# Key's rope sum moved from VectorE to GpSimd, and new orders on SyncE, ScalarE, VectorE and GpSimd in an attention block

## The reference

```python
q = einsum('bsd,ed->bse', x, Wq).reshape(bsz, seqlen, 32, 128)   # 32 query heads
k, v = ... the same with Wk, Wv, 8 key heads
q = _rope(_rmsnorm(q, q_norm_w), pos)       # rope: t * cos + swapped(t) * sin
k = _rope(_rmsnorm(k, k_norm_w), pos)
k_all = concatenate([kc, k], axis=1)        # 512 cached rows, 128 new ones
v_all = concatenate([vc, v], axis=1)
scores = where(valid, einsum('bqhd,bkhd->bhqk', q, k_all) * SCALE, -1e30)
o = einsum('bhqk,bkhd->bqhd', softmax(scores), v_all)
return einsum('bse,de->bsd', o, Wo)
```

## Time and profile before

| | |
|---|---|
| median of 3 runs | 1407.14 us (1397.35 to 1407.36) |
| profiled execution | 1401.18 us, its span 1399.4 us |
| busy in the span | PE 89%, VectorE 74%, ScalarE 60%, GpSimd 67% |
| granted TensorE clock, mean | 0.963 |

### The profile page before, as it was taken

How to read it: one execution, slowest core, us unless ns; L and a number is a source line. 1 busy time by engine, 2 the same in 40 slices (tenths; PEclk the granted TensorE clock), 3 DMA queues, 4 the chain that set the end, 5 groups by cost and what they waited for, 6 DMA issues and landing times.

```text
span 1399.4 us, 23898 instructions
## 1 busy us (share of the span) xinstructions
PE 1243.0 (89%) x6856; PEld 1012.9 (72%) x6856; DVE 1042.1 (74%) x2452; ACT 846.4 (60%) x2441; POOL 943.2 (67%) x659
## 2 busy tenths in 40 slices
PE   6799997789989999999898899899989898998878
PEld 4677765577777777777677777777767777777768
DVE  3578665587777777887787778777877788777766
ACT  2677775556665666665655566666565666565641
POOL 1566564566876788777766786688668766876652
PEclk9899999899999999999999999999999999999999
DMA  7565552446555655555555555555555555545551
GB/s 255 186 220 218 224 216 53 119 109 151 120 117 118 152 121 126 135 130 120 121 128 125 117 128 126 130 122 121 128 129 121 121 130 127 127 115 123 123 153 60
DMA packets 336036, 191.32 MB, mean 137 GB/s; under 512 B 149153, under 2 KB 320162, under 8 KB 334882
## 3 DMA queue, kind: packets, MB, share of 16 engines
q1 hardware_dynamic: 334896, 189.63, 52.5%
q10 hardware_dynamic: 1010, 0.17, 0.1%
HBM read 101.66 MB, written 37.75 MB: 100 GB/s over the span
## 4 chain that ended last, share of the span: by engine, by line
PE 29%; POOL 27%; DMA 13%; issue 9%; DVE 7%; SPq 7%; ACT 6%; DVEq 0%; POOLq 0%; ACTq 0%
POOL b_p_l L1732 13%; DMA b_moved<-b_blk_first 12%; SPq L1254 7%; PE ps L1290 4%; ACT b_p_h L1493 4%; PE ps L1291 4%; PE ps L1292 4%; POOL b_v_l L1723 4%; POOL b_ra L1719 3%; DVE b_blk_first L1608 3%; PE ps L247 2%; POOL b_w_l L1694 2%; PE ps L1358 2%; DVE b_sm L1595 2%; PE ps L306 2%
## 5 line engine op out<-in xcount | busy, mean ns | idle before, releaser
L1732 POOL TENSOR_TENSOR b_p_l<-b_moved,b_p_h 128x1280 fp32r<-128x1280 f32 x128 | 380.9, 2976 | 292.7 <-ACT b_p_h L1493 292.5
L1487 ACT ACTIVATE b_sm<-b_sm,b_mn 128x640 f32<-128x640 f32 x256 | 212.3, 829 | 98.6 <-DVE b_mn L1595 94.0
L1493 ACT ACTIVATE b_p_h<-b_moved 128x1280 fp32r<-128x1280 f32 x128 | 163.2, 1275 | 134.3 <-DMA b_moved<-b_blk_first 111.1
L1595 DVE CUSTOM_DVE_ANT_0 b_sm<-ps,mask_row,b_rstd 128x640 f32<-128x640 f32 x256 | 222.1, 868 | 7.4 <-PE ps L1292 6.7
L1290 PE MATMUL ps<-b_w_h,x1t_h 128*128 128x512 f32 (+1 forms) x512 | 190.2, 372 | 24.1 <-DVE b_qt_l L1582 24.0
L1290 PE MATMUL ps<-b_kt_h,b_qt_h 128*128 128x320 f32 x512 | 166.6, 325 | 35.4 <-DVE b_kt_l L1587 34.4
L1624 DVE SCALAR_TENSOR_TENSOR b_hacc<-ps,b_ri,b_hacc 128x512 f32<-128x512 f32 x248 | 182.7, 737 | 4.3 <-PE ps L1292 3.9
L1291 PE MATMUL ps<-b_w_l,x1t_h 128*128 128x512 f32 (+1 forms) x512 | 183.9, 359 | 0.0
L1292 PE MATMUL ps<-b_w_h,x1t_l 128*128 128x512 f32 (+1 forms) x512 | 181.8, 355 | 0.0
L1291 PE MATMUL ps<-b_kt_l,b_qt_h 128*128 128x320 f32 x512 | 158.1, 309 | 0.0
L1292 PE MATMUL ps<-b_kt_h,b_qt_l 128*128 128x320 f32 x512 | 158.0, 309 | 0.0
(11 more groups left out here) (174 smaller groups left out, 3333.4 us busy)
## 6 DMA issues: line engine op xcount, KB each, us to landing
b_moved<-b_blk_first SPq DMA_DIRECT2D x256, 160.0 KB, 3.3
b_moved<-b_blk_second SPq DMA_DIRECT2D x256, 160.0 KB, 3.3
kv_of_batch<-in_kv SPq DMA_DIRECT2D x128, 256.0 KB
b_ck<-kv_of_batch SPq DMA_DIRECT2D x64, 256.0 KB, 4.2
b_cv<-kv_of_batch SPq DMA_DIRECT2D x256, 64.0 KB, 2.3
raw<-in_w SPq DMA_DIRECT2D x32, 384.0 KB, 4.7
raw<-in_wo SPq DMA_DIRECT2D x32, 256.0 KB, 4.0
a_xt<-in_xt SPq DMA_DIRECT2D x8, 256.0 KB, 6.9
```

The costliest lines, as they stand in the source:

```text
L1487: act.activation(sm[:, h % 2], sm[:, h % 2], ACT.Exp, bias=mn[:, m.b % 2, h:h + 1], scale=-1.0, accum_out=rs[:, m.b % 2, h:h + 1]).then_in ...
L1493: act.activation(pair_of(p_h, pair), moved_pair(pair), ACT.Copy).then_inc(mh_sb, 1)
L1595: dve.tensor_tensor_reduce(sm[:, h % 2], score_row(h), mask_row[:, m.b], rstd[:, m.b % 4, h:h + 1], -MASKED, ALU.add, ALU.min, mn[:, m.b % ...
L1732: pool.tensor_tensor(pair_of(p_l, pair), moved_pair(pair), pair_of(p_h, pair), ALU.subtract).then_inc(ml_sb, 1)
```

## The change

Four edits, all in stage 2 (the first one also in the hand-over from stage 1, for item 0).

1. The key's rope sum `key_sum` leaves VectorE's list, where it stood right behind `new_values(one)`, and joins GpSimd's, behind `low_probs(last, 1)`.
2. SyncE issues `blocks_across(m, 1)` right behind `blocks_across(m, 0)`; key rows, weights and value rows come behind both.
3. ScalarE: `exponent(m, 3)` goes ahead of `output(last)`, and `new_keys(one)` and `cache_values(one)` ahead of `high(m, 0)`. VectorE: `turn_blocks(m, 3)` goes ahead of `output(last)` and `invert(last)`.
4. GpSimd: `cache_values(one)` goes ahead of `low_probs(m, 0)`.

```diff
@@ SyncE
             def slot(m, one, two, last):
                 blocks_across(m, 0)
+                blocks_across(m, 1)
                 if two:
                     key_rows(two)
...
-                blocks_across(m, 1)
                 if two:
                     value_rows(two)
@@ ScalarE
                     turned_key(one)
+                exponent(m, 3)
                 if last:
                     output(last)
-                exponent(m, 3)
-                high(m, 0)
                 if one:
                     new_keys(one)
                     cache_values(one)
+                high(m, 0)
@@ VectorE
-            def key_sum(m):
-                dve.wait_ge(kab_sb, m.n + 1)
-                dve.tensor_tensor(kb[:], ka[:], kb[:], ALU.add).then_inc(kab2_sb, 1)
...
                     new_values(one)
-                    key_sum(one)
                 minima(m, 2)
...
                 turn_blocks(m, 2)
+                turn_blocks(m, 3)
                 if last:
                     output(last)
                     invert(last)
-                turn_blocks(m, 3)
@@ GpSimd
+            def key_sum(m):
+                pool.wait_ge(kab_sb, m.n + 1)
+                pool.tensor_tensor(kb[:], ka[:], kb[:], ALU.add).then_inc(kab2_sb, 1)
...
                     low_probs(last, 1)
+                if one:
+                    key_sum(one)
                 if m.b == 6:
                     q_weights(m.g + 1, range(2, KT))
...
-                low_probs(m, 0)
                 if one:
                     cache_values(one)
+                low_probs(m, 0)
                 if two:
                     rope_queries(two)
```

More of the change, by code:

```diff
@@ L619, in x1_rest @@
                                   x1t_h[:, bass.ds(d, 1)].rearrange("p b k s -> p (b k s)"), ALU.subtract).then_inc(xl_sb, 1)
-            next_products, next_values, next_key_sum, next_queries, next_keys, next_minima, next_low_weights, next_low_kv_weights = ahead
+            next_products, next_values, next_queries, next_keys, next_minima, next_low_weights, next_low_kv_weights = ahead
             def slot(b):
@@ L678, in slot @@
                     next_values(Item(0, 0))
-                    next_key_sum(Item(0, 0))
                 if inside(b + 1):
@@ L749, in with_bias @@
                 pool.tensor_tensor(xb[:, b % 2], xin[:], b_dense[:], ALU.add).then_inc(xb_sb, 1)
-            next_q_weights, next_kv_weights, next_queries, next_rms, next_cache_keys, next_cache_values = ahead
+            next_q_weights, next_kv_weights, next_queries, next_rms, next_key_sum, next_cache_keys, next_cache_values = ahead
             def slot(b):
@@ L782, in slot @@
                     next_rms(Item(0, 0))
+                    next_key_sum(Item(0, 0))
                 if b == LAST:
@@ L1674, in low_kv_weights @@
                 dve.tensor_tensor(w_l[:, :, cols], raw[:, :, cols], w_h[:, :, cols], ALU.subtract).then_inc(wkvl_sb, 1)
-            vector_first(dve, (rope_products, new_values, key_sum, queries, new_keys, minima, low_weights, low_kv_weights))
+            vector_first(dve, (rope_products, new_values, queries, new_keys, minima, low_weights, low_kv_weights))
             slots(dve, slot)
@@ L1760, in _ @@
             pool.wait_ge(const_sb, 1)
-            gpsimd_first(pool, (q_weights, kv_weights, rope_queries, rms, cache_keys, cache_values))
+            gpsimd_first(pool, (q_weights, kv_weights, rope_queries, rms, key_sum, cache_keys, cache_values))
             slots(pool, slot)
```

## The result

The changed kernel takes 1282.82 us (median of 4 runs, 1280.65 to 1286.00); the kernel before took 1407.25 us beside it (1397.35 to 1416.34). The ratio is 0.912, with a 95% interval of 0.905 to 0.918. The profiled execution took 1286.00 us, its span 1284.2.

What follows compares the result with a forecast made beforehand. The prediction took a ring of waits (15.75 us a slot) as the bound, TensorE (14.8) right below, and VectorE's key-sum stalls third. 1401.2 - 47 (stalls) - 44 (shorter ring) = 1310 us; eight in ten between 1286 and 1352.

Steps and rivals of the forecast that it cites:

- T: Start of the four transposes of the turned queries (turn_q, line 1318) on TensorE; marks each slot in stage 2.
- ordinary slots: Stage 2 slots of batches 0, 2 to 5 and 7; forecast to fall from 15.75 to 14.8 us, 46 counted.
- Batches 1 and 6: Stage 2 slots: +0.2 us x 8 in batch 6, set by GpSimd, and -0.3 x 8 in batch 1; dropped.
- Part 1: Key sum moves from VectorE to GpSimd; its stalls behind GpSimd go and count one to one: 47 us gained.
- Part 2: Cache values go into GpSimd's idle time, new keys come earlier: 15.75 - 14.8 = 0.95 us a slot, 44 us.
- the ring: T-to-T waits: head 1's transpose, pair 0's transfers, high part, GpSimd's low part, cache values, queries' rope sum; 15.75 us.
- TensorE's floor: TensorE's own work in one of the ordinary slots, 15.75 us less holes of 0.72 and 0.24: 14.8 us.
- Part 3: SyncE issues both pairs ahead of key rows, weights and value rows; pair 1 lands 1.6 us earlier, counted as nothing.
- (b): More than forecast from pair 0's landing, batch 1's clock and batch 7: 0.4 us in 60 slots, 1286; chance 0.1.
- (a): Only the stall goes, as late transfers eat the ring's 0.3 us slack: 1354 us; chance 0.2 (up to 1358).
- (c): The stall moves to another VectorE instruction with two SBUF inputs instead of going: 1357 to 1401 us; chance 0.06.
- (d): Slower: new ring through key sum, exponent 3 and pair 1, if pair 1 lands late: 1458 us; chance 0.04.

Runs made afterwards that it cites:

- the two extra sums: Changed kernel with two more 128x128 additions on GpSimd behind the key's sum in every slot but the first, results unread: 1292.90 us, ratio 0.914.
- the orders alone: Changed kernel with the key's sum back on VectorE, all other reorderings kept: 1348.24 us, ratio 0.962 to the kernel before.
- the fastest kernel: Changed kernel with key and value weights' low part on VectorE, and batch 1's output-weight pieces moved behind GpSimd's key sum or to VectorE: 1265.47 us.

## Why the prediction was right, and where it fell short

**Where the missing 24 us are.** Between the T of item 2 and that of item 63 the prediction had 47 + 44 = 91 us, all in ordinary slots. Measured, the ordinary slots gave 106.6 us, 16 more. Batches 1 and 6, put at -1 us and dropped, gave 4. The remaining 4.5 us lie outside: 1.6 ahead of the T of item 2 and 2.8 behind that of item 63, and their cause is open.

**Part 1, the sum leaves VectorE: right.** 47 us predicted for the ordinary slots. They gave 43.9 us with the sum on GpSimd and 43.6 with one input from PSUM, against 46.5 us of stall in those slots before: nearly one to one. That the total of 48.3 us (1056.8 - 1008.5) comes so close to 47 is in part luck, since 6.4 of it is batch 1's clock. GpSimd's price, 0.48 by a line through two rows, is 0.46. That it hides in ordinary slots is shown by the two extra sums. Batch 6 pays: 18.58 to 18.85.

**Part 2, values off the ring: right mechanism, mis-sized term.** This is the step that failed: "Gain 15.75 - 14.8 = 0.95 us", 44 us in all. Measured, it is 16.02 - 14.66 = 1.36 us, 62.8 us over the 46 slots (against the run with the sum alone). Both terms were off. The split below is arithmetic on the intervals; what makes each piece is my reading of the rows.

- TensorE's floor is 14.56 us, not 14.8: 0.24 x 46 = 11 us. I subtracted the two holes that TensorE's rows print (0.72 and 0.24) and left out what a hole costs around it. After the hole of the earlier trace rows the next product is 0.38 us long and its successor starts 0.23 later; without a hole it is 0.31 and 0.14 (834.78, 834.92 above). The transposes at T took 0.66 behind a wait and 0.60 without one. And the products with the low parts, 1.20 us for four in the ordinary slot before, take 1.09 when the low part is there well ahead. In the slot before it ended at 565.54 and they began at 565.60; no idle time is printed for them. These three are 0.09, 0.06 and 0.11 us, 0.26 together. The two rows of the kernel before:

```profile
565.60 1.20 PE L1358 MATMUL ps<-b_p_l,b_v_h 128*128 128x512 f32 x4
...
572.13 0.31 PE L1291 MATMUL ps<-b_kt_l,b_qt_h 128*128 128x320 f32 x1
```

- The ordinary slot before is not 15.75. That was the best of them: the 27 ordinary slots of the kernel before whose sum did not stall average 16.04, and with the sum alone moved all 46 average 16.02. In the changed kernel the excess over the floor is 0.10, a third of 0.27. (16.02 - 15.75) - 0.10 = 0.17 x 46 = 8 us. I read it so that landings are late now and then, that the ring passes each on, and that TensorE's rate, once it binds, absorbs most of them; no run varies the landings alone. The prediction spoke of the ring's slack only as a risk; it is also where scatter disappears.

11 + 8 + 44 = 63. Less the 3 us by which part 1 fell short in the ordinary slots, that is the 16 above.

**Part 3, SyncE: "I count nothing" was wrong**, though not in the sum. I had judged it against slots of 15.75 us. There ScalarE waits for pair 1 too, but less: 21 times for 31.6 us with the sum alone moved. In slots of 14.6 pair 1 is waited for 54 times, 73 us, and putting the old order back costs 18 us. The forecast of 14.8 in the ordinary slots had tacitly used this edit. The prediction also listed the four value-row issues among those that pair 1 moves past; they stood behind pair 1 before as well. The same check on head 3 says that part of edit 3 is worth nothing, as predicted.

**Batches 1 and 6: batch 6 right, batch 1 too small.** Batch 6 takes 18.80 us, a rise of 0.22 for a predicted 0.2. Batch 1 falls by 0.71 us instead of 0.3, 5.7 us in its eight slots. Slots in which the clock stayed up fell by 0.2 only (17.10 to 16.93, two slots against five); the rest is that the clock fell in three slots instead of six, at 1.5 us each. The prediction gave this no price outside rival (b).

**The rivals.** (a) is out, since more than half of the gain is in part 2. (b) came nearest in size, 1286 against 1282.8. Its three places, pair landings, batch 1's clock and batch 7, are where the run with SyncE's old order loses its 18 us, except that pair 0's landing did not change (3.3 us) and pair 1's did; the part of it that falls in ordinary slots was already in the forecast of 14.8. (c) is out by the run with the PSUM input and the 0.45 to 0.48 us of all GpSimd sums. (d) was not seen; with the new SyncE order the high part of pair 1 waited once, for 1.1 us.

## What to carry to other kernels

When one engine takes over as the bound, it does not only cap the gain: the mean slot comes closer to the best one (0.10 us above it instead of 0.27 here). So forecast with the mean of the slots before, not with the cleanest one, and take the bounding engine's floor from products that follow each other without a break, not from a waiting slot minus its printed idle time. Two lists that feed each other have to be reordered together: GpSimd's half of the swap with ScalarE's left as it was cost 94 us, more than all the orders together gain (75 us, 1357.68 to 1282.82). And an order that seems to cost nothing in the old slot must be checked against the new, shorter one.

## What the runs showed of the hardware

A VectorE instruction with two SBUF inputs that starts behind a GpSimd instruction waits for the rest of it. The key's sum takes 0.29 us when it starts first, 2.0 us when GpSimd's low part of 2.95 us began 1.1 us earlier, up to 3.1 when it has just begun, and 0.29 in all 64 cases once one input comes from PSUM. It works both ways: GpSimd's 1.30 us instruction took 2.29 beside VectorE's 128x1024 one. The Trainium skill, page "SBUF — State Buffer", section "SBUF: two separate sides", calls it an exclusive lock held by whichever starts first; the traces agree for GpSimd's instructions on 128x512 and 128x1280.

They do not agree for its small ones. GpSimd's power of 128x5 elements for the root mean square (L1714) lasts 1.18 us and has two SBUF inputs as well. In the run with the orders alone, eight of VectorE's sums began and ended inside it; seven took 0.29 us and one, begun 0.02 us behind it, 0.32. So how long GpSimd's instruction lasts is not always how long it holds VectorE up. One of the eight:

```profile
447.78 1.18 POOL L1714 TENSOR_TENSOR b_rstd<-b_rstd,half 128x5 f32<-128x5 f32 x1
448.18 0.29 DVE L1578 TENSOR_TENSOR b_kb<-b_ka,b_kb 128x128 f32<-128x128 f32 x1
```

The race goes together with scatter of a kernel's time. Each of the ten kernels without the stalling sum stayed within 2 to 9 us over its four executions, and the one experiment with it (the orders alone) spread over 16, as the kernel before did over 19 in the first set. In many ordinary slots GpSimd's low part and VectorE's sum start within 0.03 us of each other, so a small shift decides over 2.8 us; that this is the cause of the scatter is argued and not shown.

In stage 2 the granted clock fell to the lower of its two levels in stretches of 3.4 us, in the kernel before as in the changed one. Each time TensorE had just had holes: one of 2.0 to 2.2 us, as in batches 1 and 6, or, in stalled ordinary slots, two of 0.7 and 1.2 us. Such a hole does not always bring it down, as two of the eight slots of batch 1 before show. In the fastest kernel batch 1 has no hole over 1 us, and the clock did not fall in any of its eight slots. What a fall costs depends on the slot: 1.5 us in batch 1; nothing in batch 6 with the sum alone moved, where GpSimd's list sets the slot (18.84 to 18.87 us in all seven, with the clock down in six); and 1 us in batch 6 of the fastest kernel, where GpSimd has less to do. The mean clock of the executions rose from 0.958 to 0.974 (the kernel before, all sets) to between 0.978 and 0.983 (the changed kernel). That batch 1 has three fallen slots instead of six is a count of one execution each.
